# Decays of a Mamba-2 block spread over the partitions by DMA instead of by matmuls, with the skip term and the gate product on POOL

## What is computed

```python
dt = softplus(zxbcdt[..., -NHEADS:] + dt_bias)
def step(state, inp):
    dA = exp(dt_t * A)
    state = state * dA[:, :, None, None] + (dt_t[:, :, None] * x_t)[..., None] * B_t[:, None, None, :]
    y_t = einsum('bhpn,bn->bhp', state, C_t)
y = ys + Dp[None, None, :, None] * xs
y = y * silu(z)
y = y * rsqrt(mean(y * y, axis=-1, keepdims=True) + EPS) * rms_w
```

## Time and profile before

| | |
|---|---|
| median of 3 runs | 303.43 us (301.35 to 304.26) |
| the profiled execution, its own time | 301.26 us |
| its span, first to last instruction | 299.2 us |
| busy PE / DVE / ACT / POOL | 270.4 / 247.0 / 207.6 / 105.1 us |
| mean granted TensorE clock | 0.992 |

### The profile page before, as it was taken

The page is one execution under the profiler, slowest core; times in us unless marked ns, Lnnn a source line. Parts: engine busy times, 40 slices in busy tenths (PEclk is TensorE's granted clock), DMA queues, the critical chain, the costliest instruction groups (busy, mean ns, idle before and its releaser), DMA issues.

```text
span 299.2 us, 6186 instructions
## 1 busy us (share of the span) xinstructions
PE 270.4 (90%) x2006; PEld 226.1 (76%) x2006; DVE 247.0 (83%) x537; ACT 207.6 (69%) x406; POOL 105.1 (35%) x113
## 2 busy tenths in 40 slices
PE   3999998999979999999999999997999897967781
PEld 3878996897868878887888788986798884555681
DVE  6695658787999979786899788858999999999943
ACT  1346779869868876968977787768674579777252
POOL 7000115600180614334333237116010519554552
PEclk9999999999999999999999999999999999999996
DMA  6910000000000000000000000000000100000103
GB/s 175 412 59 3 0 3 0 2 0 0 2 2 3 0 2 0 2 0 3 1 2 0 2 0 1 3 2 0 2 0 0 41 33 2 0 2 1 70 2 141
DMA packets 3787, 7.32 MB, mean 24 GB/s; under 512 B 652, under 2 KB 1581, under 8 KB 3757
## 3 DMA queue, kind: packets, MB, share of 16 engines
q1 hardware_dynamic: 3212, 6.72, 6.0%
q10 hardware_dynamic: 544, 0.21, 0.3%
HBM read 4.83 MB, written 2.10 MB: 23 GB/s over the span
## 4 chain that ended last, share of the span: by engine, by line
PE 66%; DVE 17%; issue 8%; ACT 5%; POOL 3%; DVEq 0%; ACTq 0%; POOLq 0%
PE mamba L1075 20%; PE scores L1075 17%; PE attn_out L1075 15%; PE turn L1148 7%; PE turn L1075 3%; DVE L L990 2%; DVE neg_max L900 2%; DVE th L1027 1%; DVE sp_sum L795 1%; POOL pre L524 1%; PE mamba L1166 1%; PE mamba L1207 1%; DVE L L1002 1%; DVE scanned L1010 1%; DVE res L911 1%
## 5 line engine op out<-in xcount | busy, mean ns | idle before, releaser
L1075 PE MATMUL attn_out<-values,pT 128*128 128x129 f32 x512 | 65.8, 276 | 2.5 <-DVE res L911 2.4
L1075 PEld LDWEIGHTS attn_out<-values,pT 128*128 128x128 f32 x512 | 62.2, 191 | 7.3 <-issue 4.9
L598 ACT ACTIVATE probs<-scores,neg_max 128x512 f32<-128x512 f32 x64 | 42.9, 686 | 24.6 <-DVE neg_max L900 22.2
L900 DVE TENSOR_REDUCE neg_max<-scores 128x1 f32<-128x1024 f32 x32 | 38.9, 1216 | 10.1 <-PE scores L1075 9.5
L990 DVE TENSOR_TENSOR_SCAN L<-mamba,ident 128x512 f32<-128x512 f32 x32 | 38.7, 1216 | 5.9 <-PE mamba L1075 5.7
L604 ACT ACTIVATE pT<-turn 128x512 f32<-128x512 f32 x64 | 37.6, 596 | 6.5 <-PE turn L1148 6.4
L1148 PE MATMUL turn<-ident,probs 128*128 128x128 f32 x256 | 37.9, 274 | 0.4 <-issue 0.2
L1148 PEld LDWEIGHTS turn<-ident,probs 128*128 128x128 f32 x256 | 30.2, 142 | 5.4 <-issue 3.2
L1075 PE MATMUL scores<-h_hi,q_hi 128*128 128x512 f32 x64 | 28.8, 451 | 2.7 <-ACT probs L598 1.2
L524 POOL TENSOR_TENSOR pre<-pre,th 128x512 f32<-128x512 f32 x16 | 20.7, 1292 | 27.6 <-ACT pre L630 22.2
L1075 PE MATMUL scores<-h_hi,q_lo 128*128 128x512 f32 x64 | 25.3, 395 | 0.0
(11 more groups left out here) (204 smaller groups left out, 613.9 us busy)
## 6 DMA issues: line engine op xcount, KB each, us to landing
res<-in_x_tok SPq DMA_DIRECT2D x4, 512.0 KB, 8.2
out<-res SPq DMA_DIRECT2D x8, 256.0 KB, 2.0
x_all<-in_x SPq DMA_DIRECT2D x3, 512.0 KB, 8.6
x_all<-in_x SPq DMA_DIRECT2D x2, 256.0 KB, 3.1
winT<-in_in_wT SPq DMA_DIRECT2D x1, 194.0 KB, 7.0
wqkv<-in_qkv_w ACTq DMA_DIRECT2D x1, 192.0 KB, 4.1
wpT<-in_proj_wT SPq DMA_DIRECT2D x1, 64.0 KB, 3.6
ob_row<-in_proj_b SPq DMA_DIRECT2D x1, 64.0 KB, 6.2
```

The lines of the kernel that those rows point to most:

```text
L598: act.activation(probs[:, i % 2, half_of(h)], scores[:, half_of(h)], ACT.Exp, bias=neg_max[:, i:i + 1]).then_inc(exp_done.sem, 1)
L900: V.tensor_reduce(neg_max[:, n:n + 1], scores[:, :], AX.X, ALU.max, negate=True).then_inc(max_ready.sem, 1)
L1075: return T.matmul(o, w, v, start=start, stop=stop)
```

## The change

Four parts, and a new list.

1. **The spreading.** `dA_rows`, `dA_T`, `L`, `Dec` and `decay` go. `dA` and `dec` write 32 of 128 columns of a tile that is otherwise zero, and `DAT` transposes it. A new step `rows` (ACT) copies the 32 rows out of PSUM. SP then issues `wr`, a DMA of these rows to a scratch in DRAM (16 KB); `bc`, four DMAs a half that read the four rows of a chunk back into all 128 partitions of `L` (256 KB each); and `dd`, four DMAs a half that fill `decay_in`, one per head (64 KB each). The first token's decay is made zero by a bias of -1000 before the exponential, in the place of the head mask.
2. **The scan in place.** `l` now reads `L` in SBUF and the identity in SBUF, and writes `L`. It waits for its own DMA's semaphore.
3. **The skip term** is two steps on POOL: `dx` (Dp x xs into the buffer `sq`, with the first 128 tokens straight to `yo`) and `yo_dx`, an add.
4. **The gate** is two steps on POOL, a product and an add (zt * zv, then + zv).
5. **The list** is another one throughout. SP walks it too: the stores have become steps `store` in it, and stand between `wr`, `bc` and `dd`.

```diff
+        dA = sb("dA", [P, 2, P])
+        decay_rows = sb("decay_rows", [2 * R, 2, P])
+        rows_d = nc.dram_tensor("decay_rows_d", [BATCH, 2, 2 * R, P], F32).ap()
...
+        dx = sq
...
+                if kind == "wr":
+                    wait(sp, rows_ready, b, n + 1)
+                    sp.dma_start(rows_d[b, n], decay_rows[:, n, :]).then_inc(rows_out[n].sem, 16)
+                elif kind == "bc":
+                    wait(sp, rows_out[n // QUAD], b, 16)
+                    wait(sp, filled["Y"], b - 1, n // QUAD + 1)
+                    c = n % QUAD
+                    sp.dma_start(L[:, HEADS * n:HEADS * (n + 1), :].rearrange("p h i -> p (h i)"),
+                                 rows_d[b, n // QUAD, HEADS * c:HEADS * (c + 1), :].rearrange("(a h) i -> a (h i)", a=1)
+                                 .broadcast_to([P, HALF])).then_inc(spread[n].sem, 16)
+                elif kind == "dd":
+                    wait(sp, rows_out[n], b, 16)
+                    wait(sp, yo_ready, b - 1, n + 1)
+                    for h in range(HEADS):
+                        sp.dma_start(decay_in[h * HEADDIM:(h + 1) * HEADDIM, half_of(n)].rearrange("d (c i) -> d c i", c=QUAD),
+                                     rows_d[b, n, R:2 * R, :].rearrange("(a c h) i -> h a c i", a=1, h=HEADS)[h]
+                                     .broadcast_to([HEADDIM, QUAD, P])).then_inc(decay_in_ready[n].sem, 16)
...
+                elif kind == "gate":
+                    n, part = divmod(n, 2)
...
+                    pool.tensor_tensor(gate[:, half], gate[:, half], zv[:, half], ALU.add if part else ALU.mult
+                                       ).then_inc(gate_ready.sem, 1)
...
+                elif kind == "dx":
+                    wait(pool, xs_ready, b, n + 1)
+                    wait(pool, filled["Ss"], b - 1, n + 1)
+                    wait(pool, y_ready, b - 1, n + 1)
+                    if n == 0:
+                        pool.tensor_scalar(yo[:, 0:P], xs[:, 0:P], vec[:, DP:DP + 1], 0.0, ALU.mult, ALU.add)
+                    part = slice(P, HALF) if n == 0 else half
+                    pool.tensor_scalar(dx[:, part], xs[:, part], vec[:, DP:DP + 1], 0.0, ALU.mult, ALU.add
+                                       ).then_inc(dx_ready.sem, 1)
+                elif kind == "yo_dx":
...
+                    pool.tensor_tensor(yo[:, part], yo[:, part], dx[:, part], ALU.add).then_inc(yo_dx_ready.sem, 1)
...
-                elif kind == "decay":
-                    wait(act, yo_ready, b - 1, n + 1)
-                    bank = take(act, b, "Dec", n)
-                    act.activation(decay_in[:, half], bank[:, :], ACT.Copy).then_inc(decay_ready.sem, 1)
+                elif kind == "rows":
+                    wait(act, rows_out[n], b - 1, 16)
+                    bank = take(act, b, "DAT", n)
+                    act.activation(decay_rows[:, n, :], bank[0:2 * R, 0:P], ACT.Copy).then_inc(rows_ready.sem, 1)
...
                 elif kind == "l":
-                    wait(dve, filled["Y"], b - 1, n // QUAD + 1)
-                    bank = take(dve, b, "L", n)
-                    V.tensor_tensor_scan(L[:, HEADS * n:HEADS * (n + 1), :].rearrange("p a b -> p (a b)"), bank[:, :],
-                                         ident4[:, :, :].rearrange("p a b -> p (a b)"), 0.0, ALU.mult, ALU.add
+                    wait(dve, spread[n], b, 16)
+                    chunk = L[:, HEADS * n:HEADS * (n + 1), :].rearrange("p a b -> p (a b)")
+                    V.tensor_tensor_scan(chunk, chunk, ident4[:, :, :].rearrange("p a b -> p (a b)"), 0.0, ALU.mult, ALU.add
                                          ).then_inc(l_ready.sem, 1)
```

257 lines of the change are left out of this document (111 added, 146 removed).

## The result

| | before | after |
|---|---|---|
| median | 302.39 us (301.32 to 304.26, 4 runs) | 314.84 us (313.72 to 318.2, 4 runs) |
| profiled execution, its span | 301.26, 299.2 us | 318.2, 316.5 us |
| mean granted TensorE clock | 0.992 | 0.925 |
| ratio to before | | 1.0423 [1.0318, 1.0529] |

The change makes the kernel 4.2% slower. The forecast was 292.9 us with 304 as the upper end, so even the last rival's 309.3 was too low.

The account below looks back on a forecast made before the run. PE was taken to bound 20 to 240 us, DVE 240 to 286.8. Terms -14.7 - 5.8 + 6.4 + 2.0 + 0.5 + 1.0 = -10.6 gave 290.7 us profiled, median 292.9; range 284 to 304.

Parts of the forecast that it names:

- the last rival: DVE and POOL block each other in batch d's attention and the tail; median 309.3 us at 24 meetings, chance 0.12.
- 14.7 us, in the stretch that PE bounds: `L` and `Dec` matmuls of batches a to c leave PE between 20 and 240 us; the 14.7 us count whole.
- the frame: Less PE work between 20 us and the end of attention means less time; wrong if PE idles over 25 us.
- SP spends 3.9 us a half on issues, far apart: On SP's queue, nine DMA issues a half at 0.43 us each, 3.9 us, spaced far apart.
- I count 2.0 once: Way to a scan through DRAM takes 5.2 us, 2.0 longer than before; counted only in the last half.
- the rival of the round trip: PE or DVE stands 2.5 us at the first scan in four halves; median 300.9 us, chance 0.13.
- DVE loses 5.8 and goes to 38.6: From 240 to 286.8 us DVE, still the bound, loses 5.8 us of steps and is busy 38.6.
- The meetings: DVE steps with two SBUF inputs wait for POOL: 14.6 us by chance, 6.4 counted (3.7 in DVE's stretch, 2.7 in PE's).
- 0.7 us for `dx`: On POOL, the one-input step `dx` was taken at 0.7 us each, 5.6 us in all.
- The 0.5 for `yo_dx` on the path: In the last half `yo_dx` takes 1.29 us on POOL for 0.80, on the chain to the last `y`: +0.5.
- The new list: The order differs everywhere and no row tells its effect; +1 us taken, with -3 and +6 as ends.
- the shared way: The last rival: DVE and POOL block each other over SBUF, making the kernel slower; median 309.3 us, chance 0.12.

Follow-up runs that it names:

- e9: The changed kernel with only SP's queue reordered: a quarter's four `bc` issued before `dd`, `wr` and stores; 308.06 us.
- e1: The changed kernel without the transfers through DRAM, decays left out of the result; 305.49 us, ratio 1.0045 to the kernel before.
- e13: The changed kernel with spreading transfers issued first and ten idle matmuls on PE in the last batch; 305.85 us, ratio 1.0077.
- e10: The changed kernel without transfers through DRAM (decays left out) and with ten idle matmuls on PE in the last batch; 302.81 us, ratio 0.9984.
- e16: The changed kernel with transfers issued first, ten idle matmuls, and gate and skip of all batches back on DVE; 306.45 us, ratio 1.0104.
- e15: The changed kernel without transfers (decays left out), with ten idle matmuls and all gate and skip back on DVE; 303.85 us, ratio 1.0019.
- e5: The changed kernel with ten idle 512-column matmuls added on PE in batch d's Mamba-2 block; 311.1 us, ratio 1.0191.
- e7: The kernel before with its scans reading the identity in SBUF instead of the PSUM bank, decays left out; 309.06 us, ratio 1.0156.
- e12: The kernel before with gate and skip on POOL, scans still reading PSUM; 312.96 us, ratio 1.0316.
- e8: The kernel before with scans reading the identity in SBUF (decays left out) and gate and skip on POOL; 323.26 us, ratio 1.0639.
- e17: The changed kernel with transfers issued first and ten idle matmuls, batch d's eight scans reading the identity from PSUM; 303.13 us, ratio 1.0006.
- e3: All of the change, but in the list of the kernel before; 332.23 us, ratio 1.0953.
- e18: The changed kernel with transfers first, ten idle matmuls, batch d's scans reading identity from PSUM and its gate and skip on DVE; 302.24 us.

## Why the prediction was wrong

Laid over the two stretches, the sum had -12.0 us before the end of the attention (-14.7 + 2.7) and +0.4 behind it (-5.8 + 3.7 + 2.0 + 0.5), and +1.0 for the list in neither. The traces have +1.0 and +16.3. The greater part of the miss is the tail: DVE's term there had the wrong sign. The steps that failed, in the order of the sum:

- **"24 x 0.494 + 6 x 0.470 = 14.7 us, in the stretch that PE bounds."** The work went, the time didn't. Of PE's busy time 5.4 us went, and 6.4 us of idle came in. With the queue mended (e9) 11.4 us of busy time are gone and the attention ends 9.5 us earlier. So the frame was right to two thirds, and was undone by the next point. My test for it (PE idle over 25 us) was blind: it was 14.4, and the rest hid in matmuls at a lower clock (0.97 over the stretch; at 1.00 in e9 the same matmuls are 6.0 us shorter).
- **"SP spends 3.9 us a half on issues, far apart", "I count 2.0 once".** The price of one issue stands (0.46 us for a `bc`, 0.57 for a `dd`), the rest doesn't. They are not far apart: `dd` and stores are issued between the rows and the scans that wait. Transfers and queue cost 9.4 us (e1), 6.8 of it by the queue's order (e9; the 9.4 less e13's 3.0 over e10 gives 6.4). The trip itself, well issued, costs 2.6 to 3.0 us (e16 to e15, e13 to e10), near the 2.0 I had. `bc` landed after 3.7 us where I took 2.0 to 2.5, `wr` after 1.4 where I took 2.0; the first scan came after 7.5 instead of 5.2. I had named the danger under the rival of the round trip, at 0.13, and had not looked where the list puts `dd` against `bc`, which it shows.
- **PE's clock.** No term at all. I read 1.00 in the first two stretches and took it as given, though in the second of them PE was busy only 37.8 of 46.8 us and I had just taken away 4.9 us of its work. In the tail the clock fell from 0.96 to 0.76. Ten idle matmuls give back 3.7 us (e5) or 2.7 (e10 below e1), though they are work. The clock is a follower as much as a cause: e7, e12 and e8 keep all matmuls and have 0.85, 0.84 and 0.79 in their longer tails. So the term that I lacked is not the missing matmuls alone but what any lengthening of the tail does to the clock.
- **"In the second, DVE loses 5.8 and goes to 38.6."** It stayed the busiest engine there (51.4 us against PE's 46.7), and its busy time grew. The groups show where from: stretch of 3.8 us in the eight scans (13.5 against 9.7), 1.7 in `x_all`, 1.5 in `BC`, 0.9 in `pre`, about 1 each in `xs` and `sp_den`; 3.3 us of steps that the new list has moved here (two of the four `x_all`, a `scanned`, an `xdt`); and 7.2 us gone with the change. That is +5.8 of the 8.6 measured; the rest lies in small groups, most of it in other softplus steps (`la_raw` and `sp_s` took 2.3 us more). Beside it DVE stood 7.7 us more, mostly for PE; 4.1 us of that go with e5's idle matmuls.
- **The meetings, "+6.4", 14.6 us of DVE time.** The mechanism was right: e17 shows it. That the sum of DVE time came out (225 + 14.6 = 239.6, measured 238.7) was luck. The scans brought 5.3 us over before's and not 10.2, their mean of 1.389 just under the 1.4 to 1.6, and the softplus steps together fell by about 1.5 us where I had added 4.4. Steps that I had called spared or had priced at nothing brought 11.4: the conv taps (740 to 916 ns), `BC` (686 to 1137), `x_all` (678 to 1225) and `xs` (689 to 785). And the place was wrong. I had laid a quarter into DVE's stretch; by the groups above 9.7 us lie there, about two thirds, and of the scans' 5.3 it is 3.8. The second half of the price, "what POOL loses", stood only under the rival and in no sum: POOL was forecast at 142 us, its own work is 141.7 (e12), and it took 156.5.
- **POOL's steps.** 0.7 us for `dx`: measured 0.69 undisturbed (e17) and 1.60 beside the scans (e13). The 0.5 for `yo_dx` on the path: DVE waits 1.2 us for it once in the tail. No run takes that step by itself.
- **The new list, "I take +1".** It is worth 17 us against the old one for this mechanism (e3), none of it visible as a gain, and with the queue it took 6.8.

Of the rivals, the round trip and the shared way both came true, together with the clock, for which no rival stood; I had given each a chance as if only one could. The rule of the Trainium skill, "SBUF — State Buffer", section "Who interferes with whom", that a DVE instruction with two SBUF inputs contends with a GpSimd instruction that reads SBUF, holds in this trace for large steps (5.98 against 3.43 us by one operand's place). Where the stretch that it led to is put in as measured, 9.7 us by the groups above, DVE's term in the tail is -5.8 + 9.7 = +3.9.

From 314.84 the mended causes lead down in steps: queue order 308.06, idle matmuls 305.85, identity in PSUM 303.13, last gates on DVE 302.24. Of the single steps only the third is shown by itself (e13 and e17, 12 runs each, intervals apart). The first two together are 9.0 us; how they divide is open, as e9's traced execution at 302.79 had the tail's clock at 0.88 without idle matmuls, the value that e13 has with them, and was shorter than any run of e13. The last step is within the noise.

What stays open is the 9 us between that and the forecast. In e18 the attention ends 8.4 us earlier than before and the tail is 8.9 us longer (62.0 against 53.1): DVE is busy 48.2 us in it, 5.4 more than before, and idle 13.8, 3.5 more; PE is busy 44.8. The stretch of the steps with two SBUF inputs, the steps moved there and the idle matmuls are all in it; I have not separated them further. Open too is why executions of one kernel were granted different clocks (e9: 0.942 to 0.974).

## What to carry to other kernels

Taking work from the engine that bounds one stretch helps only if the next stretch does not grow by it: here the attention's gain was given back in a tail that DVE already filled. When an operand moves from PSUM to SBUF, price the instruction anew against every large GpSimd step beside it, on both engines and where they are fullest, not spread by chance, and price the large steps that stay as they are beside the new ones too. And read a DMA queue as an engine: what waits or issues ahead of the transfer that a scan needs is on the path, whatever the transfer itself takes.
